# Lag attention: the output split into even and odd parts, both added one unit later, and the row statistics moved from VectorE to ScalarE

## What is computed

```python
x = x + tanh(g_xattn[0]) * autocorrelation(layernorm(x), ctx, ctx)

def autocorrelation(Q, K, V):       # K and V are the same tensor here
    qf = fft(q, axis=2); kf = fft(k, axis=2)
    corr = ifft(qf * conj(kf), axis=2).real
    topk = int(2 * log(L))          # 11 lags of L = 256
    w, idx = top_k(corr, topk)
    w = softmax(w)
    out = zeros_like(v)
    for i in range(topk):
        g = minimum(idx[:, :, None, :, i] + pos, L - 1)
        out = out + w[:, :, None, :, i] * take_along_axis(v, g, axis=2)
    return out
```

## Time and profile before

| | us |
|---|---|
| median of 3 runs | 1354.48 (1353.6 to 1355.89) |
| the profiled execution, whole | 1356.5 |
| its span | 1354.8 |
| lag attention within the span | 0 to about 423 |
| two units (one batch) in the middle of it, from 174.18 to 221.25 | 47.07 |

### The profile page before, as it was taken

How to read it: one execution, slowest core, us unless ns; L and a number is a source line. 1 busy time by engine, 2 the same in 40 slices (tenths; PEclk the granted TensorE clock), 3 DMA queues, 4 the chain that set the end, 5 groups by cost and what they waited for, 6 DMA issues and landing times. The chain is left out here.

```text
span 1354.8 us, 20940 instructions
## 1 busy us (share of the span) xinstructions
PE 1239.7 (92%) x6442; PEld 846.7 (62%) x6442; DVE 783.7 (58%) x2026; ACT 513.5 (38%) x939; POOL 573.0 (42%) x931
## 2 busy tenths in 40 slices
PE   4799999999878999999999998999999999968886
PEld 2354544445435954458888786988888898635443
DVE  3889999998963680015433333444554443369885
ACT  2555545454423400023322222232222322168894
POOL 5667877777642001013221222523212231068884
PEclk8999999999988899999999999999999999879998
DMA  5211212302004502227778874535333331131111
GB/s 197 92 64 32 93 62 96 138 31 109 0 1 149 224 1 84 70 85 246 265 240 283 273 233 161 187 94 128 114 103 124 96 101 54 62 70 47 62 62 78
DMA packets 52481, 156.25 MB, mean 115 GB/s; under 512 B 5952, under 2 KB 16192, under 8 KB 52288
## 3 DMA queue, kind: packets, MB, share of 16 engines
q1 hardware_dynamic: 39152, 113.46, 23.6%
q0 software_dynamic: 13264, 41.95, 10.8%
HBM read 112.93 MB, written 45.61 MB: 117 GB/s over the span
## 5 line engine op out<-in xcount | busy, mean ns | idle before, releaser
L1210 PEld LDWEIGHTS ex_bank<-ex_xT,ex_gu 128*112 128x112 f32 x1248 | 140.4, 177 | 24.3 <-issue 23.3
L1210 PE MATMUL ex_bank<-ex_xT,ex_gu 128*112 128x128 f32 x1248 | 143.6, 273 | 2.0 <-issue 1.0
L44 PE MATMUL xa_bank<-fT_high,M_hi 128*128 128x256 f32 x512 | 144.0, 281 | 0.0
L46 PE MATMUL xa_bank<-fT_high,M_lo 128*128 128x256 f32 x512 | 143.0, 279 | 0.0
L45 PE MATMUL xa_bank<-fT_low,M_hi 128*128 128x256 f32 x512 | 142.9, 279 | 0.0
L52 PE MATMUL la_bank<-la_osum,la_tab 128*128 128x512 f32 x256 | 120.8, 617 | 24.1 <-POOL la_osum L291 23.7
L291 POOL TENSOR_TENSOR la_osum<-la_oprod 128x512 f32<-128x512 f32 x64 | 80.1, 1273 | 73.7 <-DVE la_oprod L479 73.7
L1074 POOL TENSOR_TENSOR ex_small<-listed,ex_small 128x1 int32<-128x1 int32 x42 | 15.4, 368 | 223.7 <-DVE Wk L1152 223.5
L52 PEld LDWEIGHTS la_bank<-la_osum,la_tab 128*128 128x128 f32 x256 | 47.7, 196 | 86.4 <-issue 48.6
L44 PEld LDWEIGHTS xa_bank<-fT_high,M_hi 128*128 128x128 f32 x512 | 96.7, 189 | 0.3
L46 PEld LDWEIGHTS xa_bank<-fT_high,M_lo 128*128 128x128 f32 x512 | 96.7, 189 | 0.0
(11 more groups left out here) (284 smaller groups left out, 2853.4 us busy)
## 6 DMA issues: line engine op xcount, KB each, us to landing
produced<-Wk SPq DMA_DIRECT2D x39, 512.0 KB
ex_gu<-in_gate_up SPq DMA_DIRECT2D x16, 896.0 KB
X<-in_x SPq DMA_DIRECT2D x8, 1024.0 KB, 7.4
la_v_raw<-in_ctx SPq DMA_DIRECT2D x16, 512.0 KB, 4.0
produced<-la_zeros SPq DMA_DIRECT2D x16, 512.0 KB, 4.7
normal<-rt_xn SPq DMA_DIRECT2D x16, 512.0 KB, 5.4
fT<-in_ctx_T SPq DMA_DIRECT2D x8, 1024.0 KB, 5.7
xa_f<-in_ctx SPq DMA_DIRECT2D x8, 1024.0 KB, 4.8
```

The costliest lines, as they stand in the source:

```text
L44: pe.matmul(out, a[0], b[0], start=first, stop=False)
L46: return pe.matmul(out, a[1], b[0], start=False, stop=last)
L1210: m = pe.matmul(bank[half][0:INTER, 0:P], gu[:, slot, at:at + INTER], xT[:, k, :], start=(k == 0), stop=(k == KD - 1))
```

## The change

1. The tables put positions half a step off, so that the rows of tile 1 are the mirror of tile 0 with the odd terms negated. `positions(u, part)` now makes the even part (two products, bank 0) or the odd part (two products, bank 1), four in all for eight before. The lag tables are now taken at whole lags; `weight_spectra` gets two more products (six for four), and `w_halves` leaves out lag 0 and copies it in a GpSimd instruction of its own.
2. VectorE adds each part to both tiles (`add(u, b, h, part)`, the odd one to tile 1 with the negated gate `less_tg`): four adds a unit for two, all for u-2 ahead of group 2. The second two also write row sums (`accum_out`) and wait for the first two.
3. VectorE's products are split: four of `oprod` (part 0), the four of `prod`, four of `oprod` (part 1). GpSimd's sums follow the same order.
4. On TensorE `correlate` comes ahead of `positions`; three of the four products of `positions` stand ahead of the turn, the fourth behind it.
5. On ScalarE the first `lags_out` stands ahead of the last `share`.
6. From the fourth batch on (`summed_by_act`), and for all batches after the attention but the last, row statistics leave VectorE: ScalarE sums rows and squared differences (`statistic`, three places in a step, six instructions over 1024 columns and as many of one column ahead of them for each pair of units), GpSimd makes the scales from squares. Six steps instead of four are written out ahead of the loop.

```diff
-        rows_bank = [bank[4], bank[1]]
+        KINDS = (0, 3, 1, 2)
+        part_bank = [bank[0], bank[1]]
...
             def w_halves(u, g):
-                a, b = wt[:, two, 0:P], wt[:, two, P:L]
-                pool.tensor_tensor(w_less[:, two, :], a, b, ALU.subtract).then_inc(s["w_fold"], 1)
+                a, b = wt[:, two, 1:P], wt[:, two, P + 1:L]
+                pool.tensor_tensor(w_less[:, two, 1:P], a, b, ALU.subtract).then_inc(s["w_fold"], 1)
+                pool.tensor_copy(w_less[:, two, 0:1], wt[:, two, P:P + 1]).then_inc(s["w_fold"], 1)
                 pool.tensor_tensor(a, a, b, ALU.add).then_inc(s["w_fold"], 1)
...
                 if before:
-                    for i in range(4):
-                        o_sum(before[0], i)
+                    o_sum(before[0], 0)
+                    o_sum(before[0], 1)
                 if after:
                     c_sums(after[0])
+                if before:
+                    o_sum(before[0], 2)
+                    o_sum(before[0], 3)
...
+                if now and now[2] == 1 and summed_by_act(now[1]):
+                    pool.wait_ge(s["stat"], STATS * now[1] + 5)
+                    norm.on_pool_from_squares(pool, now[1] + 2)
...
+                if before and before[2] == 1 and not (fixed(before[1]) and before[1] == B - 1):
+                    at_least(pool, s["added1"], 2 * before[0] + 2)
+                    scales_after.means_on_pool(pool, before[1])
...
+                def squares(scales, b, j):
+                    act.activation(junk[:], rows(b, j), ACT.Square, bias=scales.less_mean[:, j:j + 1],
+                                   accum_out=scales.squares[:, j:j + 1]).then_inc(s["stat"], 1)
...
             def step(on, due):
                 if now:
                     exponent(now[0], 0)
+                statistic(before2, now, 0)
+                if now:
                     exponent(now[0], 1)
+                statistic(before2, now, 1)
...
                 if after:
                     spectra(after[0], True)
+                statistic(before2, now, 2)
                 if now:
                     share(now[0], 2)
                     exponent(now[0], 3)
+                if after:
+                    lags_out(after[0], 0)
+                if now:
                     share(now[0], 3)
                 if after:
-                    lags_out(after[0], 0)
                     lags_out(after[0], 1)
...
-            def add(u, b, h, j):
-                at_least(dve, s["out_pe"], 2 * u + j + 1)
-                xs = X[:, bass.ds(2 * b + j, 1), halfsl(h)]
-                dve.scalar_tensor_tensor(out=xs, in0=rows_bank[j][:].rearrange("p (a c) -> p a c", a=1), scalar=tg[:, 0:1], in1=xs,
-                                         op0=ALU.mult, op1=ALU.add).then_inc(s[f"added{j}"], 1)
+            def add(u, b, h, part):
+                at_least(dve, s["out_pe"], 2 * u + part + 1)
+                if part:
+                    at_least(dve, s["added0"], 2 * u + 2)
+                if part and h == 0:
+                    at_least(dve, scales_after.mean_ready, b)
+                for j in range(2):
+                    total = scales_after.sums[:, bass.ds(b % 2, 1), h, j:j + 1].rearrange("p o i -> p (o i)") if part else None
+                    xs = X[:, bass.ds(2 * b + j, 1), halfsl(h)]
+                    factor = less_tg if part and j else tg
+                    dve.scalar_tensor_tensor(out=xs, in0=part_bank[part][:].rearrange("p (a c) -> p a c", a=1), scalar=factor[:, 0:1], in1=xs,
+                                             op0=ALU.mult, op1=ALU.add, accum_out=total).then_inc(s[f"added{part}"], 1)
...
-                def last_rows():
+                def both_parts():
                     if before2:
+                        add(*before2, 0)
                         add(*before2, 1)
                 def products():
                     if before:
-                        o_products(before[0], before[2])
+                        o_products(before[0], 0)
                     if after:
                         c_products(after[0], after[2])
+                    if before:
+                        o_products(before[0], 1)
...
-                if before:
-                    add(*before, 0)
-                if before2 and before2[2] == 1 and not (isinstance(before2[1], int) and before2[1] == B - 1):
-                    scales_after.variance(dve, X, before2[1])
-                if due is not None:
+                if due is not None and fixed(due) and due <= 2:
                     dve.wait_ge(x_in, 16 * (due + 1))
                     norm.variance(dve, X, due)
...
-                at_least(pe, s["added0"], u)
-                full_product(pe, bank[4][:], lags_t(0), more)
-                full_product(pe, bank[5][:], lags_t(1), less).then_inc(s["wspec"], 1)
+                full_product(pe, bank[4][:], lags_t(0), more, True, False)
+                full_product(pe, bank[4][:], last_t(2), less, False, True)
+                full_product(pe, bank[5][:], lags_t(1), less, True, False)
+                full_product(pe, bank[5][:], sign_t, more, False, True).then_inc(s["wspec"], 1)
...
                 if after:
                     spectra(*after)
-                if before:
-                    positions(before[0], 0)
                 if after:
                     correlate(after[0])
+                if before:
+                    positions(before[0], 0)
+                    positions(before[0], 1, (0,))
                 if now:
                     turn_weights(now[0])
                 if before:
-                    positions(before[0], 1)
+                    positions(before[0], 1, (1,))
                 if now:
                     weight_spectra(now[0])
```

173 lines of the change are left out of this document (120 added, 53 removed).

## The result

The changed kernel takes 1379.03 us (median of 4 runs, 1377.84 to 1380.48), the kernel before it 1355.18 in the same comparison (4 runs, 1353.6 to 1357.38). The ratio is 1.0175, with a 95% interval from 1.0157 to 1.0194: the change costs 24 us. The profiled execution took 1380.48, with a span of 1378.7.

The account below looks back on a forecast made before the run. Bound: group 0's mask waits for the previous unit's turn, ScalarE's copy and exponential. Profiled execution 1356.5 + 34 for fourteen intervals - 5 at the end = 1385, 2.0 less for the median: about 1383; range 1360 to 1400.

Parts of the forecast that it names:

- Products: VectorE's products: with `prod` in between, the wait of 0.30 goes and group 3 starts at +7.3, a gain of 0.3.
- Correlations: On TensorE: their GpSimd sums are done at +6.4, and they run to +9.85, taking 3.45.
- Turn: On TensorE: waits for the weight halves, comes at +12.7 behind the unit's first product instead of +13.69, gaining 1.0.
- Turn to mask: From TensorE's turn through ScalarE's copy and exponential to VectorE's mask of group 0: 2.92 as before, mask asking at +15.6.
- Collision: VectorE's mask of group 0 waits 0.8 for GpSimd's third sum behind the weight halves; before, 0.5 on average.
- Adds: On VectorE between mask and next products: three more adds of 0.67 and a wait of about 0.35, together +2.4.
- The unit: One attention unit: 22.96 - 1.0 + 0.8 + 2.4 = 25.2, taken as 25.1, 1.6 more than 23.53.
- The clock: TensorE's idle stretches ahead of the correlations drop its clock in half the units: 0.8 a unit, bounds 0 and 1.7.
- Intervals: Fourteen intervals between products, from unit 1: 14 x (1.6 + 0.8) = 34, or 22 without the clock.
- Start: Two weight-spectra products and a slightly longer first table add 0.5 or less.
- End: Half as many position products at the end of the attention: 5 less, bounds 2 and 8.
- Statistics on ScalarE: Three instructions of about 1.23 and three small ones, 4.3 a unit, cost nothing on the path; uncovered, 1.4 each.

Follow-up runs that it names:

- The kernel with the adds in the wait: Changed kernel with the four adds ahead of group 1 instead of group 2, between group 0's last round and its mask: 1352.47 us, ratio 0.9988.
- two other kernels: Changed kernel with the spectra of Q made twice on TensorE: 1380.93 us; changed kernel with GpSimd's `q_halves` over 8 columns instead of 512: 1375.95 us.
- the one with the late copy: Changed kernel with ScalarE copying both halves of the correlations behind the last share, as before the change: 1379.05 us, ratio 1.0185.
- the positions behind the turn: Changed kernel with all four position products on TensorE behind the turn, none ahead of it: 1406.49 us, ratio 1.0383.
- the cut sums of Q: Changed kernel with GpSimd's two `q_halves` instructions over 8 columns instead of 512 from the second unit on: 1375.95 us, ratio 1.0163.
- the two fillers: Changed kernel with one extra TensorE product ahead of the correlations: 1376.21 us; the same with the spectra of Q also made twice: 1375.87 us.
- two edits: On the changed kernel: adds ahead of group 0's mask, 1352.47 us; group 0's exponential in its own tile ahead of `weights_out`, 1356.28 us; both, 1353.62 us.
- a third one: Changed kernel with early adds, group 0's exponential in its own tile, and V's first spectra right behind the turn, positions rearranged: 1337.0 us, ratio 0.9861.

## Why the prediction was right, and where its terms were off

The prediction, 1383 for a measured 1379.03, holds in its mechanism: the mask of group 0 behind turn, copy and exponential; adds that moved from free time onto the path; statistics that were filler; a clock that falls in half the units. Term by term:

- **Products.** Group 3 at +7.3 predicted, +7.18 measured. **Correlations.** +6.4 predicted, +6.39 measured; 3.45 long predicted, 3.56 at the upper clock (220.52 to 224.08).
- **Turn.** +12.7 predicted, +13.06 measured. Part of this is the prediction's sum: 7.3 + 4.03 + 1.4 is 12.7 without the 0.2 for the small copy that it names, and 12.93 with it. The weight halves do end at +12.93, since a term that was 0.2 too small, the mask at +9.60, was offset by the start of group 3 and by halves that were a little shorter. That mask takes 0.98, not 0.78 or less: at 197.49 it meets GpSimd's small copy and the sum behind it. The turn starts 0.13 behind the halves. The upper bound of 0.7 held. The positions, "level with" the weights in the prediction, end 0.4 ahead of them: the turn waits 0.38 for GpSimd.
- **Turn to mask.** 2.92 predicted, 2.97 measured (227.20 to 230.17). **Collision.** 0.8 predicted, a mask of 0.84 or 0.98 for 0.43 measured, so 0.4 to 0.55. The sum on GpSimd that it meets is the fourth, not the third, in the units in which the clock fell.
- **Adds.** 2.4 more predicted. From the first add to the next mask 3.01 (233.37 to 236.38), before 0.67 (196.29 to 196.96): 2.34 more. The kernel with the adds in the wait shows that they were on the path, though only 1.4 of it could be had in a unit without a fall.
- **The unit.** 25.1 without a fall predicted; 25.10 to 25.12 measured in the middle, 24.67 to 24.75 in the late ones. That it fits to 0.02 is partly luck: the turn was 0.36 later than predicted and the collision 0.25 to 0.4 smaller.
- **The clock.** Predicted: falls in half the units, 1.6 to 1.8 each, 0.8 a unit, 11 in all. Measured: six falls, in every second unit, at 1.15 each, 7 in all. The fall stretches the correlations by 1.69 (5.41 for 3.72), but the turn would have waited 0.38 for the weights in any case, and 1.15 reach the turn (+14.21 for +13.06) and the unit. The number of falls was right by luck in part: "half the units" was a choice between two bounds, and with the same stretch of 2.13 in each unit two other kernels had four falls in fourteen units, and the one with the late copy seven. The idle stretches were 1.5 and 2.13 for 2.2 and 2.3 predicted. The rule of the Trainium skill, page "TensorE: Matmul & The Clock Gate", section "Why this matters for your kernels", that the prediction had weighed would have kept the clock up, since it names a gap longer than any of these. The traces disagree: with one gap of 2.13 the clock fell here in every second unit over a long stretch, with 1.29 in its place in none. The row with 2.49 in the earlier trace rows had pointed the right way.
- **Intervals.** 34 predicted, 357.56 - 329.84 = 27.7 measured: 7 for the clock (11 predicted) and 21 for the rest (22). The first of them took 26.41 with no fall in it, 1.3 more than those in the middle, which the prediction had no term for: `prod` waits 1.34 for TensorE in it, and in no interval behind it.

```profile
63.96 2.48 DVE L506 TENSOR_TENSOR la_prod<-la_bank,la_v_spec 128x512 f32<-128x512 f32 x4 [1.34 <-PE la_bank L52]
```

- **Start.** 0.5 at most predicted; mark 0 of unit 1 was at 60.14 for 58.37, 1.8 later. It need not be a cost of the change: that mark was at 58.27 in the kernel with the late copy, which differs from the changed one by this copy alone, and it lay between 57.5 and 62.2 in all variants. What sets it was not looked at.
- **End.** -5 predicted; from the last of the fifteen marks to the first matmul of the router 31.25 (417.70 to 448.95) for 36.00 (388.21 to 424.21), -4.75.
- **The router's first matmuls.** No term of the sum. In the timeline of TensorE:

```profile
448.95 3.70 PE L52 MATMUL rt_bank<-X 128*128 128x512 f32 x8 [3.20 <-POOL rt_ident L887]
```

They took 3.70 for 5.21: 1.5 less, with the clock up in this execution, where the kernel with the late copy had 6.64. Together 27.7 + 1.8 - 4.75 - 1.5 = 23.3 of the 23.9 by which the span grew.

- **Statistics on ScalarE.** The waits show nothing of them on the path, as predicted, though no kernel here leaves them out; the instructions are shorter than taken (1.04 to 1.15 for 1.23), and each brings a second one of 0.18 to 0.20 that reads the accumulator:

```profile
178.68 1.13 ACT L419 ACTIVATE la_junk<-X,running_ln_small 128x1024 bf16 x1
179.72 0.19 ACT L419 ACTIVATION_READ_ACCUMULATOR la_junk<-X,running_ln_small 128x1 f32 x1
```

What was wrong were expectations of experiments, twice in the same way: each looked at one chain and did not ask how close behind it the next one was (1340 for 1352 with the adds in the wait, and 1372 for 1406 with the positions behind the turn, where an emptied stretch of TensorE cost clock as well). Three more took what is won in the units for what is won in the whole (1372 for 1376, with the cut sums of Q and with the two fillers).

## What to carry to other kernels

Work that stands where its engine waits is free, and the same work one position later in the queue can cost up to its whole length in every turn of the loop: before moving adds or statistics, find the wait of each unit and put them ahead of it. When a chain through several engines closes on itself once per unit, look for the second longest one before you promise what shortening the first brings; two edits that gave 26.6 and 22.7 us gave 25.4 together, and only a third one, on the other chain, made a faster kernel. Look at the idle stretches of TensorE that an edit leaves: a product of 0.9 us that nobody needs, put into one of 2.1, took 6 us off fourteen intervals, though of the whole time only about 3, hardly more than the scatter. And when an experiment changes the data, check that it does the same work behind the part under study: one here lost 5.5 us there, with one expert tile more to work on.

## What the runs showed of the hardware

The falls of the clock came at regular distances. In the changed kernel the stretches at 0.5 start at 144.0, 195.2, 246.4, 297.6, 348.8 and 400.0 us, 51.2 apart, and a pair of units takes 51.3; with all positions behind the turn they start in each unit, 27.3 apart, and a unit takes 27.3. With the halves of Q left out they start at 92.0, 143.2, 218.3 and 293.4, two or three units apart. In the kernels whose idle stretches stayed at 1.67 or less none came between 70 and 360 us. In the kernel with the positions behind the turn a stretch of 2.65, ahead of the turn at 127.13, was followed by none, and in the changed kernel the two of 2.2 ahead of the correlations at 93.00 and 117.76 weren't either. So a stretch of a given length (2.13) is sometimes followed by a fall and sometimes not. The even distances suggest that it matters where the stretch stands in time; that was not tested.

A mask with two inputs in SBUF took 0.42 to 0.43 alone and up to 1.58 when GpSimd was at work in SBUF at the same time, for its short instructions too (0.98 at 197.49, over the end of a copy of two columns and the sum of 0.73 behind it, which ends at 198.18). The Trainium skill, page "SBUF — State Buffer", section "🔬 SBUF: two separate sides", has the two engines exclude each other for such operations. The masks here agree: the one at 205.02 ends at 206.00, GpSimd's sum at 205.73, and the one at 230.17 at 231.01, the sum it met at 230.73; each ends 0.27 to 0.28 behind the sum.
